# The opening of a macaron block: statistics one tile ahead, the first slot's products by pairs of tiles, lowest parts and router parts ahead of the first multiplication

## The chip, the cores and the metric

One core of one Trainium2 chip. Every time is device time of one launch in microseconds (us), the median of several runs. The kernel before took 1472.89 us (three runs, 1470.03 to 1473.58).

## What is computed

The input `x` is four images of 512 rows by 512 numbers (2048 rows). Two feed-forward blocks stand around an attention block, each behind a layer normalisation and with a residual:

```python
x = x + 0.5 * ffn(layernorm(x), w12, w3, router_w, expert_bias, sw1, sw2, sw3)
x = x + attn(layernorm(x), qkv_w, conv_w0, ..., ln_b)
x = x + 0.5 * ffn(layernorm(x), ...)

def ffn(x, ...):
    shared_out = silu(x @ sw1.T) * (x @ sw2.T) @ sw3.T        # 512 -> 2048 -> 512
    scores = sigmoid(x @ router_w.T)                          # 8 experts
    _, top_idx = top_k(scores + expert_bias, 2)
    # two experts per row, 512 -> 256 -> 512 each, weighted by their scores
    return shared_out + routed_out
```

Here only the start of the first feed-forward block matters: normalising the first four row tiles, splitting the first weights, and the first products of `sw1` and `sw2`.

## The kernel before

**Numbers in two parts.** Products run in bf16, but rows and weights are split into a high and a low bf16 part, and a product takes three passes (high by high, high by low, low by high). For the router a third, lowest part of the rows is made too.

**Slots.** The shared block of one image (512 rows, four tiles of 128) is a unit of 16 slots. A slot does 128 hidden columns: 12 products of 128x128 by 128x512 into `psG` (gate), 12 into `psU` (up), then the 12 products of the slot before with `sw3` into four `psD` banks (`down`). Every engine runs its own program through the slots in the same order and meets the others only at semaphores. Slots below 0 are the preparation; `START` is -7. Slot 0 has no products down.

**One slot, engine by engine.** TensorE (PE): `products` into `psG`, `products` into `psU`, `down` of the slot before; small pieces of the side work (`sides`) stand at six fixed places between them: `pe_third` transposes the third part of a tile, `pe_logits` multiplies by the router. ScalarE (ACT): SiLU of `psG` (L1694), high part of the hidden values (L1704), high parts of rows and weights (`act_split`, L260), copies of side results (L472, L488). VectorE (DVE): the multiplication `sgh = psU * silu` (L1854), statistics, low parts of weights (`vec_split`, L265) and rows. GpSimd (POOL): low part of the hidden values (L1812) and the root of each variance (L520). SP issues nearly all transfers.

**A row tile (class `Prep`)**: `vec_stats` (three VectorE instructions, L508 to L512), `pool_rstd` (L520), `vec_norm` (for tiles 0 to 3 this is `shift`, one small VectorE instruction, L515), `act_norm` (L428), `act_high` (L436), `vec_low` (L440), then SP transposes both parts into `xT` with a DMA (`sp_cross`, L393) and keeps a copy in memory (L399). Later `vec_rest` (L446) and `vec_third` (L455) make the third part, in two VectorE passes. From tile 4 on ScalarE makes the low part (L450) from the rest. `vec_router` splits the router's weights into three parts (L504, L502).

The slots in which a tile goes through its stages stand in the table `TILE`. For tile n below 4: statistics in slot n - 7, shift and high part in n - 6, low part on VectorE in n - 5 (`preps(s - 1, HIGH)`). So VectorE does per slot: shift of one tile, statistics of the next, low part of the one before. Slots -2 and -1 hold the splits of weights 0 (gate, up, down). Then in slot 0, behind the multiplication: statistics of tile 4, router parts, split of weights 1, rest and third parts of tiles 0 and 1; tiles 2 and 3 follow in slot 1.

**TensorE in slot 0** waits for all four transposes (`crossed`) and for the gate's split, does the gate's 12 products on 512 columns each, waits for the up split, and does the other 12. In slot 1, behind the up products, `sides` wants the third part of tile 0 ahead of `down`.

**Transfers.** SP's order after the fourth transpose: weights 1 (two transfers), rows of tiles 4 and 5, the four kept copies, the first expert's weights, the store of the split weights 0, weights 2. In slot 1 it waits for the side piece of tile 0 before it loads the rows of tile 6. Weights 0 are issued by ScalarE's queue at the start.

## Time and profile before

| | |
|---|---|
| median of three runs | 1472.89 us |
| span of the profiled execution | 1469.7 us, the figure of its page |
| lowest run | 1470.03 us |
| TensorE busy | 1419.1 us (97%) |
| VectorE busy | 944.8 us (64%) |
| ScalarE busy | 552.4 us (38%) |
| GpSimd busy | 501.0 us (34%) |
| granted TensorE clock, mean | 0.998 |
| first product | 17.65 us after the start |

The span runs from the first to the last instruction of one execution; what lies around it is not in the trace, and the lowest of the three runs is 0.3 us above it. Busy times of different engines overlap. A time in a timeline counts from the start of the span. In the chain that ended last TensorE holds 63% and VectorE 10%.

### The profile page before, as it was taken

How to read it: one execution, taken by the hardware profiler on the slowest of the kernel's cores; microseconds unless marked ns; L12 is line 12 of the kernel's file. 1: busy time of each engine (PE TensorE's matmuls, PEld its weight loads, DVE VectorE, ACT ScalarE, POOL GpSimd, SP SyncE). 2: the span in 40 equal slices, each digit the busy share in tenths (PEclk: the TensorE clock that was granted, in tenths of full speed). 3: DMA queues.
4: the chain of work that ended last, by engine and by line, in shares of the span. 5: the costliest groups of instructions: out<-in, count | busy, mean ns of one | idle time of the engine just before them, and what ended most of it. 6: DMA issues, size and time to landing. Idle time of an engine off the chain costs nothing.

```text
span 1469.7 us, 22015 instructions
## 1 busy us (share of the span) xinstructions
PE 1419.1 (97%) x7642; PEld 679.7 (46%) x7642; DVE 944.8 (64%) x1295; ACT 552.4 (38%) x1153; POOL 501.0 (34%) x424
## 2 busy tenths in 40 slices
PE   4999999999999999899999999999999999999998
PEld 2444444444444544445454444444444444444443
DVE  5778853333348989898889889979925733333243
ACT  4566323333233433345435454345233213333211
POOL 2321132221244475252625434444322122221353
PEclk9999999999999999999999999999999999999999
DMA  8999659887493467075526552445338168888594
GB/s 305 305 350 320 267 146 209 200 182 192 172 277 125 156 196 220 30 244 135 153 72 186 150 166 73 121 160 140 112 101 257 59 188 213 192 190 185 187 321 165
DMA packets 233724, 272.63 MB, mean 186 GB/s; under 512 B 132242, under 2 KB 156818, under 8 KB 230162
## 3 DMA queue, kind: packets, MB, share of 16 engines
q1 hardware_dynamic: 198594, 166.34, 39.7%
q10 hardware_dynamic: 23664, 67.66, 14.5%
q0 software_dynamic: 11360, 37.23, 9.4%
q8 instruction: 66, 1.08, 0.3%
q14 instruction: 40, 0.33, 0.1%
HBM read 168.39 MB, written 72.88 MB: 164 GB/s over the span
## 4 chain that ended last, share of the span: by engine, by line
PE 63%; DVE 10%; issue 8%; DMA 4%; POOL 2%; ACT 2%; SPq 1%; POOLq 0%; ACTq 0%; DVEq 0%
PE bank L1484 25%; PE bank L1607 13%; PE bank L1498 12%; PE bank L1632 7%; DVE region L1147 3%; DMA rows<-sorted_y,slots 1%; PE side L1120 1%; PE side L1620 1%; DVE region L1153 1%; POOL rows L665 1%; DMA x2d<-rows 1%; DVE sgh L1854 1%; PE side L1253 1%; DMA region<-region 1%; POOL hs L1812 1%
## 5 line engine op out<-in xcount | busy, mean ns | idle before, releaser
L1484 PE MATMUL bank<-xT,wb 128*128 128x512 bf16 x2688 | 615.5, 381 | 22.6 <-DMA xT<-region 17.6
L1484 PEld LDWEIGHTS bank<-xT,wb 128*128 128x128 bf16 x2688 | 257.7, 98 | 323.9 <-issue 29.2
L1812 POOL TENSOR_TENSOR hs<-sgh,hs 128x512 bf16<-128x512 f32 x126 | 161.9, 1285 | 629.1 <-ACT hs L1704 628.2
L1498 PE MATMUL bank<-wb,hs 128*128 128x512 bf16 x1536 | 358.0, 380 | 0.2 <-POOL hs L1812 0.2
L1498 PEld LDWEIGHTS bank<-wb,hs 128*128 128x128 bf16 x1536 | 147.8, 98 | 173.9 <-issue 2.9
L1607 PE MATMUL bank<-wr,region 128*128 x912 | 221.7, 379 | 0.0
L1704 ACT ACTIVATE hs<-sgh 128x512 bf16<-128x512 f32 x128 | 81.3, 635 | 340.2 <-DVE sgh L1854 337.4
L1854 DVE TENSOR_TENSOR sgh<-bank,sgh 128x512 f32<-128x512 f32 x128 | 87.9, 687 | 155.8 <-PE bank L1484 154.6
L1147 DVE TENSOR_TENSOR region<-region 128x1024 f32<-128x1024 f32 x128 | 183.0, 1454 | 0.9
L1801 POOL DMA_INDIRECT region<-xnd,idxs x78 | 74.6, 957 | 221.8 <-DMA region<-region 213.5
L1153 DVE TENSOR_REDUCE region<-region 128x256 f32<-128x2048 f32 x64 | 146.3, 2286 | 2.2
L1694 ACT ACTIVATE sgh<-bank 128x512 f32<-128x512 f32 x128 | 76.4, 597 | 183.3 <-PE bank L1484 164.3
L1607 PEld LDWEIGHTS bank<-wr,region 128*128 128x128 bf16 x912 | 86.0, 98 | 89.8 <-issue 0.7
L1632 PE MATMUL bank<-wr,region 128*128 x468 | 113.7, 379 | 0.0
L1951 DVE TENSOR_TENSOR region<-bank,region 128x256 f32<-128x256 f32 x76 | 32.3, 425 | 97.8 <-ACT region L1742 88.7
L665 POOL DMA_INDIRECT rows<-sorted_y,slots x64 | 67.9, 1062 | 78.5 <-issue 73.4
L1742 ACT ACTIVATE region<-bank 128x256 f32<-128x256 f32 x76 | 29.2, 384 | 172.2 <-PE bank L1607 167.8
L1484 PE MATMUL bank<-region,wb 128*128 128x512 bf16 x384 | 85.9, 379 | 1.9 <-DVE sgh L1854 1.9
L1961 DVE COPY region<-side 128x512 bf16<-128x512 bf16 x78 | 33.1, 425 | 83.5 <-PE side L1620 83.5
L1632 PEld LDWEIGHTS bank<-wr,region 128*128 128x128 bf16 x468 | 45.8, 98 | 55.2
L686 DVE SCALAR_TENSOR_TENSOR rows<-rows,coef 128x512 f32<-128x512 f32 x32 | 26.2, 820 | 68.7 <-DMA rows<-sorted_y,slots 28.3
L1484 PEld LDWEIGHTS bank<-region,wb 128*128 128x128 bf16 x384 | 37.4, 98 | 47.3 <-DVE sgh L1854 2.4
(182 smaller groups left out, 1351.6 us busy)
## 6 DMA issues: line engine op xcount, KB each, us to landing
wb<-wsplit ACTq DMA_DIRECT2D x42, 1024.0 KB
wb<-wsplit ACTq DMA_DIRECT2D x42, 512.0 KB, 4.4
sorted_y<-region SPq DMA_DIRECT2D x78, 256.0 KB
wsplit<-wb SPq DMA_DIRECT2D x8, 1536.0 KB, 7.4
wr<-wall SPq DMA_DIRECT2D x6, 1536.0 KB, 9.7
rows<-x SPq DMA_DIRECT2D x32, 256.0 KB, 4.9
region<-xln SPq DMA_DIRECT2D x128, 64.0 KB, 3.7
xnd<-rows SPq DMA_DIRECT2D x30, 256.0 KB, 4.0
```

The lines of the kernel that those rows point to most:

```text
L665: e.indirect_dma_start(out=dst, out_offset=None, in_=sorted_y, in_offset=bass.IndirectOffsetOnAxis(ap=slots[:, self.f, k, self.t:self.t + ...
L1147: o.do(e.tensor_tensor(t, few.to_broadcast(full), many.to_broadcast(full), ALU.mult))
L1153: o.do(e.tensor_reduce(dst[:, (k - 1) * P:(k + 1) * P], self.tmp.rearrange("p (n c) -> p n c", c=H), AX.X, ALU.add))
L1484: m = e.matmul(ps[:], wb[:, w % 2, wp, at:at + P], xt[:, xp, c, :], start=(i == 0), stop=(i == 3 * NDC - 1))
L1498: m = e.matmul(psD[tt][:], hs[:, s % 2, hp, tt * P:(tt + 1) * P], wb[:, w % 2, wp, at:at + D], start=(first and i == 0), stop=(last and i ...
L1607: m = e.matmul(psH_of(k)[:], xsT[k % RX][:, xp * D + c * P:xp * D + (c + 1) * P], words_of(k, wp, c * D), start=(n == 0), stop=(n == 3 * N ...
L1632: m = e.matmul(psY[k % 2][:], hT[k % 2][:, hp, kt, :], words_of(k, wp, at), start=(n == 0), stop=(n == 3 * KT - 1))
L1694: e.activation(sgh[:, s % 2, :], psG[:], ACT.Silu).then_inc(S("h_silu").sem, 1)
L1704: e.activation(hs[:, s % 2, 0, :], sgh[:, s % 2, :], ACT.Copy).then_inc(S("h_hi").sem, 1)
L1801: e.indirect_dma_start(out=xs[k % RX], out_offset=None, in_=xnd, in_offset=bass.IndirectOffsetOnAxis(ap=idxs[:, k:k + 1], axis=0)).then_in ...
L1812: e.tensor_tensor(hs[:, s % 2, 1, :], sgh[:, s % 2, :], hs[:, s % 2, 0, :], ALU.subtract).then_inc(S("h_lo").sem, 1)
L1854: e.tensor_tensor(sgh[:, s % 2, :], psU[:], sgh[:, s % 2, :], ALU.mult).then_inc(S("h_mul").sem, 1)
```

## The change

It touches TensorE's and VectorE's programs only. TensorE gets `opening()` in the place of slot 0: for gate and up, the products of tiles 0 and 1 (256 columns), then those of tiles 2 and 3, each pair with its own wait for the transposes (once, with the gate) and 12 matmuls; the waits for the splits stay. That makes 48 matmuls of 256 columns out of 24 of 512. VectorE gets `opening()` in the place of the slots below 0: the statistics of tile n + 1 stand ahead of the shift of tile n (tile 3's behind the shift of tile 2), and the rest and third parts of tiles 0 and 1 and the router parts stand behind the splits of weights 0, ahead of slot 0's multiplication, no longer in slot 0. The slots of ScalarE, GpSimd and SP are unchanged.

```diff
--- before.py
+++ after.py
@@ -1486,6 +1486,24 @@
                             i += 1
                     m.then_inc(S(name).sem, 1)
 
+                def opening():
+
+                    for gu, ps, name in ((0, psG, "h_g"), (1, psU, "h_u")):
+                        e.wait_ge(S("w_low").sem, split_done("gu"[gu], 0))
+                        for pair in range(2):
+                            two = slice(2 * pair * P, 2 * (pair + 1) * P)
+                            if gu == 0:
+                                for n in (2 * pair, 2 * pair + 1):
+                                    crossed(e, n)
+                            i = 0
+                            for c in range(NDC):
+                                for wp, xp in PASSES:
+                                    at = gu * NDC * HC + c * HC
+                                    m = e.matmul(ps[:, two], wb[:, 0, wp, at:at + P], xT[0][:, xp, c, two],
+                                                 start=(i == 0), stop=(i == 3 * NDC - 1), skip_group_check=True)
+                                    i += 1
+                        m.then_inc(S(name).sem, 1)
+
                 def down(s, tt):
                     w, k = chunk(s), s % 2
                     first, last = s == 0 or s in EV_AT, s + 1 in EV_AT
@@ -1542,6 +1560,9 @@
                         for pos in range(6):
                             sides(s, pos)
                         return
+                    if s == 0:
+                        opening()
+                        return
                     if s % UNIT == 0:
                         for n in range(4 * u, 4 * u + 4):
                             crossed(e, n)
@@ -1549,25 +1570,22 @@
                             e.wait_ge(S("x_moved").sem, 16 * (u - 1))
                     if s % 2 == 0:
                         if s < UNIT:
-                            e.wait_ge(S("w_low").sem, split_done("gu" if s else "g", chunk(s)))
+                            e.wait_ge(S("w_low").sem, split_done("gu", chunk(s)))
                         elif s % UNIT >= 2 * KT:
                             q, v = chunk_loaded(u, s % UNIT // KT)
                             e.wait_ge(S(f"gu_loaded{q}").sem, v)
                     if s in ROUTED_AT:
                         e.wait_ge(S("r_mul").sem, NB * (ROUTED_AT.index(s) + 1) - 1)
-                    elif s:
+                    else:
                         e.wait_ge(S("h_silu").sem, s)
                     products(psG, s, 0, "h_g", 0)
                     if s in ROUTED_AT:
                         block[ROUTED_AT.index(s)][0](NB - 1)
                     sides(s, 1)
-                    if s == 0:
-                        e.wait_ge(S("w_low").sem, split_done("u", 0))
-                    else:
-                        e.wait_ge(S("h_mul").sem, s)
+                    e.wait_ge(S("h_mul").sem, s)
                     products(psU, s, 1, "h_u", 2)
                     sides(s, 3)
-                    behind = s > 0 and s not in ROUTED_AT
+                    behind = s not in ROUTED_AT
                     if behind:
                         down_ready(s - 1)
                         down(s - 1, 0)
@@ -1847,11 +1865,32 @@
                 e.wait_ge(S("ident_ready").sem, 1)
                 routing = [None, None]
 
+                def opening():
+
+                    tiles = [Prep(n) for n in range(4)]
+                    tiles[0].vec_stats(e, o)
+                    tiles[1].vec_stats(e, o)
+                    tiles[0].vec_norm(e)
+                    tiles[2].vec_stats(e, o)
+                    tiles[1].vec_norm(e)
+                    tiles[0].vec_low(e)
+                    tiles[2].vec_norm(e)
+                    tiles[3].vec_stats(e, o)
+                    tiles[1].vec_low(e)
+                    tiles[3].vec_norm(e)
+                    tiles[2].vec_low(e)
+                    tiles[3].vec_low(e)
+                    for kind in ("g", "u", "down"):
+                        vec_split(e, kind, 0)
+                    for n in range(2):
+                        tiles[n].vec_rest(e)
+                        tiles[n].vec_third(e)
+                    vec_router(e)
+
                 def slot(s):
-                    if s >= 0:
-                        e.wait_ge(S("h_silu").sem, s + 1)
-                        e.wait_ge(S("h_u").sem, s + 1)
-                        e.tensor_tensor(sgh[:, s % 2, :], psU[:], sgh[:, s % 2, :], ALU.mult).then_inc(S("h_mul").sem, 1)
+                    e.wait_ge(S("h_silu").sem, s + 1)
+                    e.wait_ge(S("h_u").sem, s + 1)
+                    e.tensor_tensor(sgh[:, s % 2, :], psU[:], sgh[:, s % 2, :], ALU.mult).then_inc(S("h_mul").sem, 1)
                     if s in ROUTED_AT:
                         e.wait_ge(S("h_hi").sem, s + 1)
                         e.tensor_tensor(hs[:, s % 2, 1, :], sgh[:, s % 2, :], hs[:, s % 2, 0, :],
@@ -1885,24 +1924,17 @@
                     for c in combines(s):
                         if c.ln:
                             c.vec_norm(e)
-                    for p in preps(s - 1, HIGH):
-                        if p.n < 4:
-                            p.vec_low(e)
-                    if s == 0:
-                        vec_router(e)
-                    if s >= 0:
-                        for p in preps(s, LOW):
-                            if p.early:
-                                p.vec_rest(e)
+                    for p in preps(s, LOW):
+                        if p.early:
+                            p.vec_rest(e)
                     for kind, n in splits_at(s)[:1]:
                         vec_split(e, kind, n)
-                    if s >= 0:
-                        for p in preps(s, LOW):
-                            if p.early:
-                                p.vec_third(e)
+                    for p in preps(s, LOW):
+                        if p.early:
+                            p.vec_third(e)
                     for kind, n in splits_at(s)[1:]:
                         vec_split(e, kind, n)
-                    for n in (0, 1) if s == 0 else (2, 3) if s == 1 else ():
+                    for n in (2, 3) if s == 1 else ():
                         Prep(n).vec_rest(e)
                         Prep(n).vec_third(e)
                     for f in range(2):
@@ -1967,7 +1999,8 @@
                         hidden(k)
                     hidden_T(NB - 1)
 
-                for s in range(START, SLOTS_ALL):
+                opening()
+                for s in range(SLOTS_ALL):
                     if s in ROUTED_AT:
                         routed(ROUTED_AT.index(s))
                     slot(s)
```

## Rows read from the trace of the kernel before

**Rows 1.** The page: busy time of TensorE, and its costliest group of weight loads

```profile
...
PE 1419.1 (97%) x7642; PEld 679.7 (46%) x7642; DVE 944.8 (64%) x1295; ACT 552.4 (38%) x1153; POOL 501.0 (34%) x424
...
L1484 PEld LDWEIGHTS bank<-xT,wb 128*128 128x128 bf16 x2688 | 257.7, 98 | 323.9 <-issue 29.2
...
```

**Rows 2.** Waits of TensorE, 0 to 47 us: total, times, longest

```profile
...
PE side L481 <- ACT rows L472: 2.1, 1, 2.1
PE side L463 <- DVE rows L455: 2.1, 1, 2.1
```

**Rows 3.** Timeline of all engines: start, duration, instruction [idle before, releaser]

```profile
...
3.79 0.69 DVE L508 BATCH_NORM_STATS2 stats<-rows 128x6 f32<-128x512 f32 x1 [3.79 <-DMA rows<-x]
...
4.74 0.15 DVE L512 TENSOR_SCALAR mv<-mv 128x1 f32<-128x1 f32 x1
4.98 0.57 POOL L520 TENSOR_TENSOR rstd<-mv,nhalf 128x1 f32<-128x1 f32 x1 [3.19 <-DVE mv L512]
5.59 0.16 DVE L515 SCALAR_TENSOR_TENSOR mv<-mv,rstd 128x1 f32<-128x1 f32 x1 [0.69 <-POOL rstd L520]
...
8.53 0.68 DVE L440 TENSOR_TENSOR rows<-rows 128x512 bf16<-128x512 f32 x1
8.69 0.93 POOL L520 TENSOR_TENSOR rstd<-mv,nhalf 128x1 f32<-128x1 f32 x1 [1.29 <-DVE mv L512]
...
11.87 0.16 DVE L515 SCALAR_TENSOR_TENSOR mv<-mv,rstd 128x1 f32<-128x1 f32 x1 [0.44 <-POOL rstd L520]
...
12.06 0.81 ACT L428 ACTIVATE rows<-rows,mv,rstd 128x512 f32<-128x512 f32 x1 [0.74 <-DVE mv L515]
12.74 2.78 SPq L393 DMA_TRANSPOSE xT<-region  x2
...
13.45 2.93 ACT L260 ACTIVATE wb<-region 128x1024 bf16<-128x1024 f32 x3
13.57 0.69 DVE L440 TENSOR_TENSOR region<-rows,region 128x512 bf16<-128x512 f32 x1 [0.94 <-ACT region L436]
14.52 3.50 DVE L265 TENSOR_TENSOR wb<-region,wb 128x1024 bf16<-128x1024 f32 x3 [0.25 <-ACT wb L260]
...
17.65 12.64 PE L1484 MATMUL bank<-xT,wb 128*128 128x512 bf16 x48 [17.65 <-DMA xT<-region]
...
```

**Rows 4.** The same timeline: weight loads of the first products

```profile
...
18.03 0.15 PEld L1484 LDWEIGHTS bank<-xT,wb 128*128 128x128 bf16 x1 [0.27 <-issue]
...
21.87 7.92 PEld L1484 LDWEIGHTS bank<-xT,wb 128*128 128x128 bf16 x37 [0.28 <-issue]
...
```

**Rows 5.** The same timeline: slots 0 to 2

```profile
...
25.21 0.69 DVE L1854 TENSOR_TENSOR sgh<-bank,sgh 128x512 f32<-128x512 f32 x1 [7.20 <-PE bank L1484]
...
28.64 2.28 DVE L265 TENSOR_TENSOR wb<-region,wb 128x2048 bf16<-128x2048 f32 x1
...
33.50 0.68 DVE L1854 TENSOR_TENSOR sgh<-bank,sgh 128x512 f32<-128x512 f32 x1
...
35.51 1.45 PE L1484 MATMUL bank<-xT,wb 128*128 128x512 bf16 x6
...
41.48 0.69 DVE L1854 TENSOR_TENSOR sgh<-bank,sgh 128x512 f32<-128x512 f32 x1 [1.67 <-PE bank L1484]
...
43.26 1.89 ACT L260 ACTIVATE wb<-region 128x2048 bf16<-128x2048 f32 x1
...
43.55 1.07 DVE L446 TENSOR_TENSOR rows<-rows 128x512 f32<-128x512 f32 x1
...
45.06 0.61 ACT L450 ACTIVATE rows<-rows 128x512 bf16<-128x512 f32 x1
...
```

**Rows 6.** Transfers issued from 22.7 to 23.4 us: size, us to landing

```profile
...
region<-wall SPq DMA_DIRECT2D x1, 512.0 KB, 16.4
```

**Rows 7.** Transfers issued from 32.7 to 33.1 us (tile 6)

```profile
...
rows<-x SPq DMA_DIRECT2D x1, 256.0 KB, 7.0
```

**Rows 8.** Timeline of VectorE, from 75 us: statistics of tile 10

```profile
...
81.18 0.69 DVE L508 BATCH_NORM_STATS2 stats<-rows 128x6 f32<-128x512 f32 x1 [2.11 <-issue]
...
```

## The prediction

> **What bounds the kernel now.** I read the page first: TensorE is busy for 1419.1 of 1469.7 us [rows 1], so the time is its idle time plus its work, and only what moves TensorE counts. The waits of TensorE in the first 47 us came second: 2.1 us for the third part of a row tile (L463) and 2.1 us for ScalarE's copy of one (L472) [rows 2], beside the 17.65 us until the first product, whose row shows it waiting for a transpose [rows 3]. That is 21.9 of some 50 us of idle time, and the change touches all three. Then I read the timeline of that stretch on each engine [rows 3, 5], the weight loads of the first products, for the clock [rows 4], and the landing of the transfers that could come late next [rows 6 to 8].
>
> **The opening up to the first product.** Each of the four tiles goes VectorE statistics, GpSimd root, VectorE shift, ScalarE normalise and high part, VectorE low part, transpose by SP. The statistics take 1.03 us (3.79 to 4.74, and 0.08 until the next can start); the root then holds VectorE up for 0.69 us [rows 3]. Now the next tile's statistics fill that wait. Followed with these rows:
> - Statistics 0 from 3.79, 1 from 4.82, shift 0 at 5.84 instead of 5.59: the first tile is 0.25 us later, ScalarE starts at about 6.03 (0.19 after a shift, as 11.87 to 12.06). GpSimd, ScalarE and SP keep the order of their own work; each only meets its waits earlier.
> - Normalise and high part hold ScalarE for 1.39 us (12.06 to 13.45). Shifts 1 and 2 fall at 6.94 and 8.15, so ScalarE runs 6.03, 7.42, 8.81 with no gap.
> - VectorE: low part 0 at 7.54 (1.51 after its normalise, as 12.06 to 13.57), statistics 3 from 8.23, low part 1 at 9.25. Root 3 starts beside low part 1 and takes 0.93 instead of 0.57 us, as the one at 8.69 did beside the low part at 8.53; shift 3 falls at 10.38, normalise 3 at 10.58 instead of 12.06.
>
> So the last low part and the three weight splits come 1.48 us earlier: 12.09 and, on VectorE, 13.04 instead of 13.57 and 14.52. If root 2, which starts 0.45 us ahead of low part 0, is held up by it too, this shrinks to 1.0 us; above 1.5 us nothing is left, since ScalarE has no gap. I take 1.48: root 2 has most of its 0.57 us behind it by then.
>
> Products by pairs. Now TensorE waits for all four transposes: the last issue is at 14.29 (12.74 + 2.78 - 1.23) and the first product at 17.65, 3.36 later [rows 3]. With pairs it needs tiles 0 and 1 (low part 1 done at 9.94, issued 9.97, landed about 13.3) and the first split (13.04 + 3.50/3 = 14.2). Start: 14.27. The second pair is needed 12 half products later, 16.8; tile 3 is issued at 12.8 and lands at 16.1. Gain at the start: 1.48 + 1.90 = 3.38 us.
>
> Cost of halving: 24 products of 512 columns become 48 of 256. The slot's 24 products took 4.22 + 14 x 0.216 = 7.25 us, 7.29 with the change of clock, and still do if the clock rises 4.2 us after the start again. The first slot ends at 21.6 instead of 24.9.
>
> **What moves ahead of the first multiplication on VectorE.** Rest and third parts of tiles 0 and 1 took 2.6 us (from the split's end, 30.92, to the next multiplication, 33.50), the router parts up to 1.8 us (28.64 - 25.21 less the multiplication and one set of statistics) [rows 5]. They now follow the splits, 16.55 to about 20.9, with VectorE idle there before, and end 0.9 us ahead of the multiplication at 21.8, which waits for TensorE. If the cover goes, the multiplication is late one for one, but the second slot's first half (2.6 us) stands between it and TensorE. Behind it: statistics of tile 4, whose rows had landed by 25.8 and now 1.5 earlier, then the split of the second weights, 3.43 us after the multiplication as before, 25.2 to 27.5. Second multiplication at 27.5. TensorE: slot 1's 24 products take 5.2 us and end at 26.74. Before, they ended at 30.1 and slot 2 began at 35.51; of these 5.4 us 2.3 are the wait for the third part with its restart, 3.1 are work (transposes, products down, logits). The third part is ready from 18 on, so slot 2 starts at 29.85. **Difference 5.66 us** = 3.38 + 2.28 (the wait and its restart). Slot 2 needs the split by then: 2.3 us spare. Its parts 2 and 3 are ready at about 33.7, before TensorE asks.
>
> **Slot 2, where I take some back.** The third wait is a chain behind the multiplication at 41.48: ScalarE high part, weight split (43.26), low part of tile 4 (45.06), copy, TensorE at about 46.3 [rows 2, 5]. It stays, 5.66 earlier, if nothing else is late. VectorE reaches the statistics of tile 6 at 36.9. That tile's load was issued at about 32.8 and landed 7.0 later, 39.8 [rows 7], 0.7 us behind the second part of weights 2 (22.7 + 16.4 = 39.1) [rows 6]. Those weights are issued 1.48 earlier and land at 37.6, early enough for the split at 37.6; the tile's load, though issued at 27.4, stands behind them: 38.3. Statistics end at 39.3, rest part 4 at 40.0 (0.7 like a low part; its 1.07 at 43.55 began beside GpSimd's work, which is over by then), and ScalarE, free at 39.4, starts the low part at 40.0: **0.62 us lost**. If the load took 7.0 us from its issue it would land at 34.4 and nothing would be lost; if it stayed at 39.8, 2.1 us would be.
>
> The Trainium skill, DMA: Bandwidth & Descriptors, section Queues, rings and completion order, says that each engine takes one queue's descriptors in ring order: by that the sum loses the 0.62 us, without it nothing. The 0.7 us between the two landings is what speaks here for order.
>
> **Sum.** 3.38 + 2.28 - 0.62 = 5.04 us earlier at slot 3. From there TensorE is nearly without idle time, and what follows hangs on the slots. The new waits are those of the pairs; behind them on TensorE stand only the same products. Against the profiled execution: span 1469.7 - 5.0 = 1464.7. The three runs have the median 1472.9, 3.2 above that span; I subtract from the median: 1467.9.
>
> **Rivals.**
> 1. *A later clock.* The price is half of each further us at 1.2 GHz; if all 28 remaining half products run low, 28 x 0.107 = 3.0 us, gain 2.0, 1470.9. For it: an earlier start with shorter products. Against: 4.2 us of dense work was enough in [rows 4] and is there again. Chance 0.11. The Trainium skill, TensorE: Matmul & The Clock Gate, Part 1, says that the number of products at half rate differs from run to run of one kernel, which is this rival; one trace cannot test it.
> 2. *The transfers set the pace.* Loads come 1.48 us earlier, work 5.0: up to 3.5 us of queue can stand ahead of slot 3. Tile 10's rows already held VectorE for 2.1 us [rows 8], so what is left of it then goes one for one; together with tile 6 at 39.8 the gain is 1.5 to 3.5, 1469.4 to 1471.4. Against: 6 slots in between. Chance 0.14.
> 3. *The pairs do nothing*, since transposes 0 and 1 slow down beside the first weight load and land with the others: 1.90 lost, gain 3.1, 1469.8. Chance 0.07.
> 4. *Slower.* A gap between the pairs (transpose 3 after 16.8) keeps the clock low. The half-rate stretch costs half its length, so from 10.1 us more of it, a rise after 28.6, the gain is gone; if it stays low to the end of slot 2 the loss is 3.0 + 24 x 0.214 + 36 x 0.214 = 15.8, less 5.0: 1483.7. Against: transpose 3 has 0.7 us spare. Chance 0.05.
> 5. *More*: later waits shrink too, or no loss in slot 2, 1465 to 1467.2. Chance 0.06.
>
> **Numbers.** My forecast has 0.57 and by itself 1466.4 to 1469.4. About 0.3% (4.4 us, 1468.5) is what a measurement of this kernel can tell from no change. Of the forecast's 0.57, 0.44 lies beyond that and 0.13 within; with rival 5 faster is 0.50. Rivals 1 to 3 (0.32) and a hundredth of 4 lie within: 0.46. Slower: 0.04. The range leaves out most of 4 and the ends of 1, 2 and 5, and allows for the 3.5 us by which the three runs differ: 1464.5 to 1472.
>
> **What would show it.** First product at 14.3 with starts 0.21 us apart, the first multiplication at 21.8, the last low part at 12.1. TensorE's wait for L455 gone, that for L472 at 2.7 instead of 2.1 us, and VectorE waiting about 1.4 us for tile 6's rows. Tile 10's wait still about 2.1. The prediction is wrong if the first product starts after 15.5, if the half-rate stretch exceeds 5 us, or if a later wait of TensorE grows by over 1 us.

## The result, and the profile after

The kernel after took 1470.78 us (median of 20 runs, 1465.47 to 1473.95) where the kernel before, on the same chips, took 1474.5 us (20 runs, 1469.81 to 1479.72): a ratio of 0.9975, 95% interval [0.9967, 0.9983], 3.7 us or 0.25%. That is beyond chance, but under the 0.3% named ahead. 5.0 us were predicted.

The page of after and its row of cores (TensorE's granted clock averaged over the span), beside [rows 1]:

```profile
span 1470.5 us, 22063 instructions
...
PE 1422.8 (97%) x7666; PEld 683.9 (47%) x7666; DVE 942.7 (64%) x1295; ACT 552.2 (38%) x1153; POOL 497.4 (34%) x424
...
core 0: 1470.5 us, clock 0.995
```

The profiled execution of after is 0.8 us *longer* than that of before (1469.7 us, clock 0.998). Two single executions can't be set against each other at their ends; they can be at the opening, where the change lies. Waits of TensorE in the first 47 us (total, times, longest), beside [rows 2]:

```profile
PE bank L1502 <- DVE wb L265: 14.3, 1, 14.3
PE side L481 <- ACT rows L472: 3.2, 1, 3.2
```

The wait for the third part (L455) is gone, the start comes 3.35 us earlier, and the last wait has grown by 1.1 us. The timeline of the opening, beside [rows 3]:

```profile
4.81 0.69 DVE L508 BATCH_NORM_STATS2 stats<-rows 128x6 f32<-128x512 f32 x1
...
5.82 0.15 DVE L515 SCALAR_TENSOR_TENSOR mv<-mv,rstd 128x1 f32<-128x1 f32 x1
...
7.06 0.55 POOL L520 TENSOR_TENSOR rstd<-mv,nhalf 128x1 f32<-128x1 f32 x1 [0.52 <-DVE mv L512]
...
8.23 3.86 SPq L393 DMA_TRANSPOSE xT<-rows  x2
...
9.36 0.93 POOL L520 TENSOR_TENSOR rstd<-mv,nhalf 128x1 f32<-128x1 f32 x1 [1.76 <-DVE mv L512]
...
10.33 0.16 DVE L515 SCALAR_TENSOR_TENSOR mv<-mv,rstd 128x1 f32<-128x1 f32 x1 [0.44 <-POOL rstd L520]
...
12.03 0.69 DVE L440 TENSOR_TENSOR region<-rows,region 128x512 bf16<-128x512 f32 x1 [0.94 <-ACT region L436]
12.14 2.69 SPq L393 DMA_TRANSPOSE xT<-region  x2
12.98 3.50 DVE L265 TENSOR_TENSOR wb<-region,wb 128x1024 bf16<-128x1024 f32 x3 [0.26 <-ACT wb L260]
...
14.30 5.07 PE L1502 MATMUL bank<-xT,wb 128*128 128x256 bf16 x23 [14.30 <-DVE wb L265]
...
14.87 0.58 SPq L278 DMA_DIRECT2D region<-wall  x1
```

Every VectorE step stands within 0.1 us of the hand-worked schedule (5.84, 10.38, 12.09, 13.04), and so does the first product (14.27): root 3 took its 0.93 us beside a low part, root 2 escaped with 0.55. SP does not follow: two transposes occupied it from 8.23 to 12.09, in before from 9.24 to 12.70, so the first load behind the transposes went out at 14.87, only 0.70 us earlier (15.57 before) instead of 1.48. By the second part of weights 2 SP has made that up (21.21 against 22.72). The first two transposes landed 5.0 and 4.2 us after their issue (3.1 and 3.2 in before), the second at about 14.1, just ahead of the first product.

One thing on the clock. The granted clock reads 1.00 all through this opening, in before too, so its level there is read from the distance of the starts alone. Slots 0 to 3, beside [rows 5]:

```profile
18.43 0.69 DVE L455 TENSOR_TENSOR rows<-rows 128x512 bf16<-128x512 f32 x1
...
22.46 0.69 DVE L1893 TENSOR_TENSOR sgh<-bank,sgh 128x512 f32<-128x512 f32 x1 [2.35 <-PE bank L1502]
...
30.48 1.45 PE L1484 MATMUL bank<-xT,wb 128*128 128x512 bf16 x6
...
36.45 0.69 DVE L1893 TENSOR_TENSOR sgh<-bank,sgh 128x512 f32<-128x512 f32 x1 [2.29 <-PE bank L1484]
...
39.41 0.69 DVE L508 BATCH_NORM_STATS2 stats<-rows 128x6 f32<-128x512 f32 x1 [1.81 <-issue]
...
41.14 0.63 ACT L450 ACTIVATE rows<-rows 128x512 bf16<-128x512 f32 x1 [1.01 <-DVE rows L446]
...
42.40 0.20 PE L481 MATMUL side<-rw,xT 128*128 128x24 bf16 x2 [3.24 <-ACT rows L472]
...
43.90 0.15 PEld L1484 LDWEIGHTS bank<-xT,wb 128*128 128x128 bf16 x1 [0.23 <-issue]
...
44.32 0.15 PEld L1484 LDWEIGHTS bank<-xT,wb 128*128 128x128 bf16 x1 [0.28 <-issue]
...
50.36 0.69 DVE L1893 TENSOR_TENSOR sgh<-bank,sgh 128x512 f32<-128x512 f32 x1 [6.45 <-PE bank L1484]
```

VectorE waits 1.81 us for the rows of tile 6 (39.41), and TensorE 3.24 us for what hangs on them. It goes on at 42.40, 3.9 us ahead of before. Then something unforeseen: from 43.90 its weight loads start 0.42 us apart, the 1.2 GHz level, until 46.88, so the multiplication of slot 3 comes only 2.2 us earlier (50.36 against 52.58). Two transfers, beside [rows 6, 7] (size, us from issue to landing; the weights were issued at 21.21, the rows at 27.78):

```profile
region<-wall SPq DMA_DIRECT2D x1, 512.0 KB, 17.5
...
rows<-x SPq DMA_DIRECT2D x1, 256.0 KB, 11.5
```

They land at 38.7 and 39.3 us, 0.6 us apart (0.7 in before) and only 0.4 and 0.5 us earlier than there. Three later waits:

```profile
79.36 0.20 PE L481 MATMUL side<-rw,xT 128*128 128x24 bf16 x2 [1.17 <-issue]
...
96.57 0.69 DVE L508 BATCH_NORM_STATS2 stats<-rows 128x6 f32<-128x512 f32 x1 [1.80 <-issue]
...
97.48 0.20 PE L481 MATMUL side<-rw,region 128*128 128x24 bf16 x2 [1.38 <-issue]
```

The first is TensorE in slot 6, waiting for the transpose of tile 7, issued at 72.48 and landed 6.8 us later; before has it too (1.34 us). The second is VectorE, waiting 1.80 us for the rows of tile 12 (0.32 in before, though they come 0.9 us earlier now: the work asks 2.4 us earlier). The third is new: TensorE in slot 8, waiting for the transpose of tile 9, issued at 89.15 and landed 8.2 us later (6.8 in before, without a wait). All the way, from the start times of the multiplications in both timelines:

```
multiplication at (before)   25.2   33.5   41.5   52.6   96.0   112.8   182.6
earlier in after by           2.75   5.65   5.0    2.2    2.4     1.1     1.1
```

### The profile page after: what moved, and what is told of

Its sections match the earlier page's. It is cut to its first block, busy times and chain, and to the rows that moved or that the text cites. A ratio compares the mean times of both kernels' runs of the same rounds, so it can differ in the third digit from the quotient of the medians.

```text
span 1470.5 us, 22063 instructions
## 1 busy us (share of the span) xinstructions
PE 1422.8 (97%) x7666; PEld 683.9 (47%) x7666; DVE 942.7 (64%) x1295; ACT 552.2 (38%) x1153; POOL 497.4 (34%) x424
## 4 chain that ended last, share of the span: by engine, by line
PE 64%; DVE 10%; issue 8%; DMA 4%; POOL 2%; ACT 2%; SPq 1%; POOLq 0%; ACTq 0%; DVEq 0%
PE bank L1484 25%; PE bank L1625 13%; PE bank L1516 13%; PE bank L1650 7%; DVE region L1147 3%; DMA rows<-sorted_y,slots 2%; PE side L1120 1%; PE side L1638 1%; DVE region L1153 1%; POOL rows L665 1%; DVE sgh L1893 1%; PE side L1253 1%; DMA region<-region 1%; PE side L1236 1%; DVE rows L578 0%
## 5 line engine op out<-in xcount | busy, mean ns | idle before, releaser
L1484 PE MATMUL bank<-xT,wb 128*128 128x512 bf16 x2664 | 609.4, 380 | 5.2 <-ACT sgh L1712 3.7
L1993 DVE COPY region<-side 128x512 bf16<-128x512 bf16 x78 | 33.1, 425 | 83.7 <-PE side L1638 83.7
```

The costliest lines, as they stand in the source:

```text
L1484: m = e.matmul(ps[:], wb[:, w % 2, wp, at:at + P], xt[:, xp, c, :], start=(i == 0), stop=(i == 3 * NDC - 1))
```

## Experiments

A1 to A4 ask what closes in at the end of slot 2, B1 to B3 undo one part of the change each, C to E follow up what these left open. All were timed against before on the same chip. Ratios are of medians, with their 95% intervals.

**A1. TensorE kept at work.** After, plus twelve products that nobody reads, in the gate's bank, just ahead of the side work it waits with. Nothing is left out.

```diff
                         down(s - 1, 3)
+                    if s == 2:
+                        e.wait_ge(S("h_silu").sem, 3)
+                        for i in range(12):
+                            e.matmul(psG[:], xT[0][:, 0, 0, 0:P], xT[0][:, 0, 0, :], start=(i == 0), stop=(i == 11))
                     sides(s, 5)
```

> The changed kernel with 12 products more that nobody reads, into the gate's bank at the end of slot 2, where TensorE waits 3.2 us for ScalarE's copy of tile 2's third part (12 x 0.216 = 2.6 us, so they end before the wait does). Clock theory (that wait lets TensorE's clock fall for 3.4 us, 1.7 us lost): no stretch at 0.50 near 44 us, the copy still ends the wait near 42.4, slot 3's multiplication on VectorE at 48.7 instead of 50.4, median 1.7 us below the changed kernel, some 0.9963 of the kernel before. Rival (the clock there costs nothing, since slot 3 is held by loads): slot 3's multiplication stays at 50.4, ratio 0.9975.

1469.67 us (12 runs), ratio 0.9969 [0.9958, 0.998]. Stretches of after (us, busy time and instructions of PE, PEld, VectorE, ScalarE, GpSimd; then the granted clock, the DMA's share and GB/s):

```profile
43.90:44.90 1.00, 1.00 (x4) 0.45 (x3) 0.01 (x1) 0.00 (x0) 0.00 (x0) 0.50 0.77 164
44.90:45.90 1.00, 1.00 (x4) 0.30 (x3) 0.00 (x0) 0.00 (x0) 0.00 (x0) 0.50 1.07 263
```

The same of A1, and its TensorE row behind the products:

```profile
43.90:44.90 1.00, 1.00 (x6) 0.49 (x5) 0.13 (x1) 0.00 (x0) 0.00 (x0) 1.00 0.77 161
44.90:45.90 1.00, 1.00 (x10) 0.57 (x8) 0.00 (x0) 0.23 (x1) 0.00 (x0) 1.00 1.12 302
```

```profile
42.52 0.20 PE L481 MATMUL side<-rw,xT 128*128 128x24 bf16 x2 [1.88 <-ACT rows L472]
```

TensorE goes on at the same moment (42.52 against 42.40) but at the full clock, and the multiplication of slot 3 comes at 48.80 instead of 50.36, 6.28 us behind that moment instead of 7.96: the half-rate stretch costs 1.7 us, and no more. That the products kept the clock up isn't shown by one profile; behind B1's wait of 3.13 us, without such products, it stayed up as well. The median lies 1.1 us below after's, within the two intervals.

**A2. Tile 6's rows ahead of weights that aren't needed yet.** SP loads the first expert's weights (1.5 MB) behind those rows; weights 2 stay ahead of them.

```diff
                             Prep(n).sp_keep(e)
-                        load_raw(e, NU)
...
+                    if s == 1:
+                        load_raw(e, NU)
                     for n in raws_at(s):
```

> The changed kernel with the first expert's weights (1.5 MB) issued in slot 1 behind tile 6's rows, instead of ahead of the store of split weights 0. Queue theory (tile 6's rows land late because they stand behind what was issued before): 1.5 MB less ahead of them at 0.4 MB per us, so they land near 35.7 instead of 39.3, before VectorE asks at 37.5; its wait of 1.8 us goes, TensorE's wait at the end of slot 2 falls from 3.2 to 2.1 us, and the fall of the clock with it where the shorter wait is not seen by the clock: 1.1 us, or 2.8 us with the clock, ratio 0.9956 to 0.9967. Rival (the load's own latency under load is what counts): it lands 11 us after its issue as before, nothing moves, 0.9975. Tiles 7 and 10 must not come later than before (VectorE's wait in slot 6 stays 1.9 us).

1468.45 us (6 runs), 0.9954 [0.9939, 0.9969]. Its timeline:

```profile
37.22 0.68 DVE L508 BATCH_NORM_STATS2 stats<-rows 128x6 f32<-128x512 f32 x1
...
40.98 0.20 PE L481 MATMUL side<-rw,xT 128*128 128x24 bf16 x2 [2.11 <-ACT rows L472]
...
47.25 0.69 DVE L1894 TENSOR_TENSOR sgh<-bank,sgh 128x512 f32<-128x512 f32 x1 [4.49 <-PE bank L1485]
```

VectorE no longer waits, TensorE's wait is 2.11 us again, the clock holds. Weights 2 land at 34.7 us (issued at 20.00, 14.7 us) and the rows at 35.3 (27.49, 7.8 us), still 0.6 us behind them. With 1.5 MB less ahead of the rows the late opening of slot 3 goes: what stood ahead of them in the queue was the cap.

**A3. The router products of tile 2 out of TensorE's way**, from slot 2 into slot 3.

```diff
-                logits_at = ((1, 5), (2, 2), (2, 5), (3, 2))[n]
+                logits_at = ((1, 5), (2, 2), (3, 1), (3, 2))[n]
```

> The changed kernel with tile 2's router products moved from the end of slot 2 to behind the gate products of slot 3. If the copy on ScalarE is all that TensorE waits for there, the wait of 3.2 us goes and the clock stays high: slot 3's multiplication comes 3.2 + 1.7 = 4.9 us earlier, at 45.5 instead of 50.4. Transfer theory (the loads then become the bound): part of it comes back as waits of VectorE for the rows of tiles 7, 8 and 10, up to what TensorE has gained, and the median falls by less than 3 us; without it by 4 to 5 us (0.9942 to 0.9948 of the kernel before).

1468.03 us (6 runs), 0.9951 [0.9935, 0.9968]. Its timeline:

```profile
45.48 0.69 DVE L1893 TENSOR_TENSOR sgh<-bank,sgh 128x512 f32<-128x512 f32 x1 [1.95 <-PE bank L1484]
...
57.78 0.69 DVE L508 BATCH_NORM_STATS2 stats<-rows 128x6 f32<-128x512 f32 x1 [2.46 <-issue]
...
58.33 0.20 PE L481 MATMUL side<-rw,xT 128*128 128x24 bf16 x2 [1.85 <-issue]
...
60.04 0.15 PEld L1484 LDWEIGHTS bank<-xT,wb 128*128 128x128 bf16 x1 [0.24 <-issue]
60.47 0.15 PEld L1484 LDWEIGHTS bank<-xT,wb 128*128 128x128 bf16 x1 [0.28 <-issue]
```

The slot-3 multiplication comes 4.9 us ahead of after, as expected (45.5), and two slots on most of it is gone: TensorE waits 1.85 us, and its clock drops behind that (starts 0.43 us apart). In slot 5 the lead over after is 1.4 us. What ends the wait at 58.33 is the transpose of tile 5, issued at 50.40, which lands at 58.2:

```profile
xT<-rows SPq DMA_TRANSPOSE x1, 7.8
```

Tile 8's rows hold VectorE for 2.46 us, but not TensorE: it goes on 0.55 us behind the start of their statistics, where after needed 3.0 us from such a start to what is made from it (39.41 to 42.40).

**A4. Both, A2 and A3.**

> Both moves, of the first expert's load and of tile 2's router products, in the changed kernel. Clock and queue theory together: as with the router products moved alone, and VectorE does not wait for tile 6 in slot 2 either; since TensorE no longer hangs on it there, this adds little over the other (0 to 1 us): 0.994 to 0.995 of the kernel before. If the transfers are the bound from slot 3 on, the gain of both is no more than that of either alone.

1468.9 us (6 runs), 0.9955 [0.9939, 0.9971]. The slot-3 multiplication stands at 44.55. In slot 4 TensorE waits 2.45 us for the transpose of tile 5 (issued at 48.38, landed 9.5 us later), and the clock falls again: no better than either alone. Tile 8's rows, 3.06 us late, hold only VectorE. Under the first cap lies a second, and it is a transpose.

**B1. The statistics back behind the shift** (the rest of the change kept).

```diff
                     tiles[0].vec_stats(e, o)
-                    tiles[1].vec_stats(e, o)
                     tiles[0].vec_norm(e)
-                    tiles[2].vec_stats(e, o)
+                    tiles[1].vec_stats(e, o)
                     tiles[1].vec_norm(e)
+                    tiles[2].vec_stats(e, o)
                     tiles[0].vec_low(e)
```

> The changed kernel with VectorE's statistics back behind the shift of the tile before. Step theory: the last low part and the splits come 1.48 us later again, first product at 15.8 instead of 14.3 us; the loads that SP issues behind the fourth transpose come later too. Clock theory adds that the stretch at half rate behind it differs by run. Slot 3's resume 1.5 us later, unless the wait for tile 6's rows hides it (then less, since those rows move only with SP's loads); median 0 to 1.5 us above the changed kernel, ratio 0.9975 to 0.9985 of the kernel before.

1472.16 us (12 runs), 0.9983 [0.9969, 0.9996]. The first product moves from 14.30 to 15.80, which is the 1.5 us worked out for this part. The end of slot 2 moves from 42.40 to 44.01, since here the loads behind the transposes are later too (the first at 15.53 instead of 14.87).

**B2. No pairs**: all four transposes first, then products of 512 columns.

```diff
-                        for pair in range(2):
-                            two = slice(2 * pair * P, 2 * (pair + 1) * P)
-                            if gu == 0:
-                                for n in (2 * pair, 2 * pair + 1):
-                                    crossed(e, n)
+                        if gu == 0:
+                            for n in range(4):
+                                crossed(e, n)
+                        for pair in range(1):
+                            two = slice(0, 4 * P)
```

> The changed kernel with slot 0's products on 512 columns behind all four transposes. Step theory: first product 3.2 to 3.4 us behind the fourth transpose's issue (13.5 us), near 16.8; slot 2's multiplication 2.5 us later, near 39. Tile 6's rows land at 39.3 either way and are asked for at 40 then, so VectorE's wait of 1.8 us goes, TensorE waits 2.1 instead of 3.2 us at the end of slot 2 and resumes near 43.7, 1.3 us after the changed kernel, not 2.5. If the shorter wait also keeps the clock up, the pairs bring nothing at all: slot 3's multiplication at 50.0 against 50.4, ratio 0.997 to 0.998.

1470.62 us (12 runs), 0.9965 [0.9952, 0.9978]. Its timeline:

```profile
16.62 0.59 PE L1502 MATMUL bank<-xT,wb 128*128 128x512 bf16 x1 [16.62 <-DMA xT<-region]
...
42.95 0.20 PE L481 MATMUL side<-rw,xT 128*128 128x24 bf16 x2 [2.12 <-ACT rows L472]
```

The pairs are worth 2.3 us at the first product and 0.55 at the end of slot 2. The wait there is 2.12 us, the clock doesn't fall, and slot 3's multiplication (49.22) is even ahead of after's. Nothing of the pairs can be seen in the time.

**B3. Rest, third and router parts back in slot 0.**

```diff
                         vec_split(e, kind, 0)
-                    for n in range(2):
-                        tiles[n].vec_rest(e)
-                        tiles[n].vec_third(e)
-                    vec_router(e)
...
+                    if s == 0:
+                        vec_router(e)
...
-                    for n in (2, 3) if s == 1 else ():
+                    for n in (0, 1) if s == 0 else (2, 3) if s == 1 else ():
```

> The changed kernel with the rest and third parts of tiles 0 and 1 and the router parts back in slot 0, behind its multiplication. Step theory: TensorE's wait of 2.1 us for the third part (L455) comes back in slot 1, slot 2 starts 2.3 us later (32.8 instead of 30.5), and slot 2's multiplication comes at 38.7. As with the pairs, the wait for tile 6 then shrinks, so of the 2.3 us some 1.1 us or less are left at the end of slot 2, and with the clock up nothing. Ratio 0.997 to 0.9985; the rival, that every microsecond of slot 2 counts in full, gives 2.3 us above the changed kernel, 0.999.

1471.49 us (12 runs), 0.9977 [0.9963, 0.9991]. Its timeline:

```profile
28.70 0.38 PE L463 MATMUL side<-identb,rows 128*128 128x128 bf16 x4 [2.10 <-DVE rows L455]
...
42.60 0.20 PE L481 MATMUL side<-rw,xT 128*128 128x24 bf16 x2 [2.12 <-ACT rows L472]
```

The 2.1 us wait is back, and yet the end of slot 2 moves by 0.2 us alone: what is won ahead of tile 6's rows is waited away at them. Part of the 0.2 is luck, since the clock rose at 17.7 here and at 20.0 in after; against D3 (18.1, the end at 42.30) it is 0.3.

**C. Tiles 10 to 15 loaded one slot earlier**, on top of A2.

```diff
-            TILE.append((n - 5 if n >= 6 else None, at, ...
+            TILE.append((n - 6 if n >= 10 else n - 5 if n >= 6 else None, at, ...
```

> The changed kernel with the first expert's load behind tile 6's rows, and the rows of tiles 10 to 15 loaded one slot earlier. Queue theory: VectorE's waits for tile 10 (1.9 to 2.1 us) and tile 12 (1.3 to 1.8 us) go, and TensorE's two waits behind them (1.3 and 1.1 us): 2.4 us below the version with the first expert's load alone moved, 0.9935 to 0.9945 of the kernel before. Rival: the queue is full there, so the rows come at the expense of the weights, VectorE or ScalarE waits for those instead, and the ratio stays 0.9954.

1469.42 us (12 runs), 0.9959 [0.9945, 0.9973]. VectorE's waits for tiles 10 and 12 are gone, TensorE's small waits in slots 6 and 8 are not (2.8 us together), and nothing is won over A2. They end when a transpose lands, 7.0, 6.7 and 8.6 us after its issue. So the rows of tile 10 [rows 8] are not what holds TensorE.

**D1. Stores of the split weights on ScalarE's queue**, on top of A2: do the transposes get free of them?

```diff
-                    if 0 <= s < UNIT and s % 2 == 0:
-                        store_split(e, s // 2)
...
                         act_split(e, kind, n)
+                    if 0 <= s < UNIT and s % 2 == 0:
+                        store_split(e, s // 2)
```

> The changed kernel with the first expert's load behind tile 6's rows, and the stores of the split weights issued on ScalarE's queue instead of SP's. TensorE's waits of 1.2 to 1.4 us in slots 6 and 8 end where the DMA transposes of tiles 7 and 9 land, 6.8 and 8.2 us after their issue. Queue theory (a transpose waits for what stands ahead of it on SP's queue): 1.5 MB less ahead, they land in 3 to 5 us, both waits go, 2.4 us below the version with the first expert's load alone moved: 0.9935 to 0.9945 of the kernel before. Rival (all queues share the same 16 engines, so the transposes land no sooner): the waits stay, 0.9954.

1470.75 us (12 runs), 0.9975 [0.9964, 0.9987]: no gain; tile 7's transpose still takes 6.3 us, those of tiles 8 to 10 take 7.5 to 8.0. Its end of slot 2, and a stretch behind it (columns as above):

```profile
40.60 0.20 PE L481 MATMUL side<-rw,xT 128*128 128x24 bf16 x2 [2.12 <-ACT rows L472]
```

```profile
42.00:43.00 1.00, 1.00 (x4) 0.42 (x3) 0.38 (x1) 0.00 (x0) 0.00 (x0) 0.50 0.49 182
```

Here the clock fell behind a wait of only 2.12 us.

**D2. The statistics alone** (B2 and B3 together): are the two parts each other's spare?

> The changed kernel with both the pairs and the early rest, third and router parts undone; only the statistics ahead are left. If tile 6's rows (landed at 39.3) cap slot 2, each of the two parts alone brings TensorE nearly as far as both: it resumed at 42.4 with both, at 42.6 without the early parts, at 42.95 without the pairs. Without both nothing is capped: 1.0 to 1.5 us before the kernel before, at 44.8 to 45.3, slot 3's multiplication at 51.1 to 51.6. Sum theory (parts add): 42.4 + 0.2 + 0.55 = 43.2. Median 1 to 1.5 us below the kernel before, ratio 0.999 to 0.9993.

1472.13 us (12 runs), 0.9982 [0.9971, 0.9994]. Its timeline:

```profile
30.69 0.38 PE L463 MATMUL side<-identb,rows 128*128 128x128 bf16 x4 [2.11 <-DVE rows L455]
...
44.59 0.20 PE L481 MATMUL side<-rw,xT 128*128 128x24 bf16 x2 [2.11 <-ACT rows L472]
```

The end of slot 2 stands at 42.40 with both parts, 42.95 and 42.60 without one, 44.59 without either. Each alone is worth 1.6 to 2.0 us there, both together 2.2: they add almost nothing to each other, because the cap lies at 42.4. The median is 2.6 us below before's, where 1 to 1.5 were expected.

**D3. The kernel after again**, for how much one profile tells.

> The changed kernel once more, on the chip of the others, for a second trace: statistics of tile 6 again held to 39.0 to 39.6 us, TensorE resumes at 42.2 to 42.6. By the clock theory the stretch at half rate behind that wait of 3.2 us comes again (near 44); if it was chance it is not there and slot 3's multiplication comes at 48.7. Tile 12's rows late by over 1 us again, and TensorE's waits at the landing of the transposes of tiles 7 and 9. Ratio 0.9975 within 0.0012.

1470.74 us (12 runs), 0.9975 [0.9963, 0.9987], the first result again. Its timeline:

```profile
42.30 0.20 PE L481 MATMUL side<-rw,xT 128*128 128x24 bf16 x2 [3.89 <-ACT rows L472]
...
43.01 0.15 PEld L1484 LDWEIGHTS bank<-xT,wb 128*128 128x128 bf16 x1 [0.28 <-issue]
43.43 0.15 PEld L1484 LDWEIGHTS bank<-xT,wb 128*128 128x128 bf16 x1 [0.28 <-issue]
```

In the opening the clock rose 1.9 us earlier than in the first profile (18.1 against 20.0), and slot 2's multiplication stood at 35.70 instead of 36.45. But the end of slot 2 is the same (42.30 against 42.40), the wait only longer, and the fall of the clock is there again.

**E. A2 and eight unread products** behind slot 2, nothing left out: does the pair beat both?

> The changed kernel with the first expert's load behind tile 6's rows, and 8 products that nobody reads (1.7 us) in the 2.1 us in which TensorE then waits at the end of slot 2. With both the late rows and the fall of the clock gone: rows of tile 6 never waited for, TensorE resumes 0.6 us behind the last filler where it resumed without them (40.6 to 41.5), no stretch at 0.50 near 42 us, slot 3's multiplication 6.3 us after the resume (46.9 to 47.8), ratio 0.995 (0.9938 to 0.9962), 3 to 4 us below the changed kernel. If the clock falls behind such a wait only now and then (one look in six so far), the fillers add 0.3 us at most over the move alone, 0.9954.

1469.53 us (12 runs), 0.9968 [0.9956, 0.9979], not the 0.995 hoped for. Its opening:

```profile
15.01 8.04 PE L1503 MATMUL bank<-xT,wb 128*128 128x256 bf16 x48 [15.01 <-DMA xT<-rows]
```

The first product waited for a transpose until 15.01, 0.8 us later than A2's (14.25), and the clock rose late (20.6). TensorE went on at 41.98, and slot 3's multiplication came at 48.25, a microsecond behind A2's; the whole microsecond is there at the first multiplication already (23.16 against 22.16). The products fill the wait of 2.1 us down to 0.39; that is worth something only where the clock would have fallen, and in A2 it hadn't. Whether A2's load order is worth anything over after isn't settled either: E contains it and lies 1.3 us below after, C 1.4, D1 nothing, all within each other's intervals.

**The profiles together.** The lead over the profile of before at the multiplication that stands at 182.6 us there (worked out from the start times), the lead of the medians, what the span of each profile adds to its lead behind 182.6 us, and how many half-rate stretches the granted clock shows from 183 us to the last microseconds (before: 2; one of B2's is twice as long and counts as two):

```
                     D2   after  B1   D1   D3   B2   A1   B3   E    C    A3   A4   A2
lead at 182.6 us     0.8  1.1    1.6  1.7  2.0  2.5  3.0  3.1  3.4  3.5  3.9  4.2  4.4
lead of the medians  2.6  3.7    3.2  3.9  4.0  4.8  5.2  3.9  4.8  6.0  6.8  5.9  6.4
behind 182.6 us     -4.3 -1.9   -0.5 -3.1  1.8 -2.1 -2.5 -3.1 -0.8 -0.5 -3.0 -2.7 -1.8
half-rate stretches  3    3      2    3    1    3    3    4    2    2    3    3    2
```

The first two go together (correlation 0.90, slope 0.99, 2.0 us between them). So do the last two (correlation -0.86, 1.8 us for each stretch, beside the 1.7 that A1 gives for one): what moved the single profiles behind 183 us, in code that the change doesn't touch, is mostly how often the clock fell there.

## Why the prediction was right, and where it wasn't

1. **The opening, 3.38 us: right.** First product at 14.30 (14.27 forecast), each VectorE step within 0.1 us. B1 puts 1.5 us on the statistics. B2 gives the pairs 2.3 us of the first product, where 1.9 stood. It was close: the second transpose landed at 14.1, not at 13.3, and in D1 and E TensorE waited for it until 15.0, which is rival 3 in part.
2. **Halving at no cost, clock after 4.2 us: the first held, the second didn't.** The half products start 0.21 us apart at 1.2 GHz. B2, with whole products, needs 7.5 us from the first product to the first multiplication, 4.2 of them at the low clock, and after 8.2, of them 5.7: the 0.7 between them is half of the longer stretch, and nothing is left for the halving. But in the first profile the clock rose 5.7 us after the start instead of 4.2, slot 0 took 8.05 us instead of 7.29, and the first multiplication came at 22.46, not 21.8. That is rival 1, by 0.75 us. It costs nothing in the end: D3, 0.75 us ahead in slot 2, ends it at the same time.
3. **The wait for the third part: right.** It is gone, the moved VectorE work is done at 20.1 us, ahead of the multiplication, and B3 and D2 bring the wait back at 2.1 us.
4. **Tile 6's rows, 0.62 us: right in kind, too small.** They land behind the weights, at 39.3. The term is mis-sized in "those weights are issued 1.48 earlier and land at 37.6". Their second part was issued 1.51 earlier (21.21 against 22.72), but took 17.5 us instead of 16.4 and landed at 38.7, 0.4 earlier. Two transfers ahead of it kept their lead: the first expert's weights landed 1.7 us earlier (19.45 + 10.6 against 20.76 + 11.0), the store of weights 0 1.6. What made weights 2 slower isn't shown. TensorE loses 1.1 us more. That the rows land behind what stands ahead of them in the queue is shown: 0.7 us behind weights 2 in before and 0.6 in after, D3 and A2, from 7.0 to 12.2 us after their own issue. The Trainium skill, DMA: Bandwidth & Descriptors, section Queues, rings and completion order, has an engine consume descriptors in ring order. The trace agrees with that.
5. **"What follows hangs on the slots": wrong.** The longer wait at the end of slot 2 is followed by a half-rate stretch in both profiles of after (1.7 us by A1). I had put the risk of the clock into the opening, not behind the wait that the change itself makes longer. It isn't certain: the clock fell behind 3.24 and 3.89 us, not behind B1's 3.13; behind waits of about 2.1 us at that place it fell in one of seven profiles (D1), and stayed up in before, A2, B2, B3, C and D2. Two slots on it fell behind 1.85 us (A3) and 2.45 us (A4).
6. **Rival 2, later loads: it happened, in part.** Slots 8 to 10 give 1.3 us back, nearly all of it in the new wait of 1.38 us at 97.48. My reading of [rows 8] was wrong: it is a wait of VectorE that TensorE doesn't feel (C). TensorE's own waits there, and in slot 4 of A3 and A4, end where a transpose lands; the prediction has no transpose behind the opening.
7. **The sum.** 5.04 less 1.1 (tile 6), 1.7 (clock) and 1.1 (net, behind slot 3) is 1.1, the lead in the first profile at 182.6 us. The medians lie 3.7 apart. The profile of before is a quick one: its span of 1469.7 us stands for a launch of about 1471.4 (in every timed run the launch time is 1.7 to 1.8 us above the span), 3.1 below the median of 1474.5. Whether the 2.0 us between the two kinds of lead are luck that it already had at 182.6 us, or whether the other kernels win them behind that, one profile of before can't show. So 1470.78 falls inside the range of 1464.5 to 1472.0, but outside the likeliest case's own (1466.4 to 1469.4), near what rivals 1 and 2 gave. Of the 2.9 us above the forecast of 1467.9, 1.6 come from its base, since the median of three runs (1472.89) was 1474.5 in twenty, and 1.3 from the gain. The gain was forecast beyond 0.3% with chance 0.50 and within it with 0.46; it lies within.
8. **Its own signs of being wrong.** Of the three that it names, the first didn't come (the first product started at 14.3). The other two did: the half-rate stretch was 5.7 us in the first profile (3.7 in D3), over the 5 named, and the wait for L472 grew by 1.1 us, over the 1 named, beside the new wait of 1.38. The total held better than the account of what follows slot 2, and that part of it is luck.

That slot 3 comes only 2.2 us earlier is therefore mostly a cap: the pairs and the early third parts win 1.6 to 2.0 us each alone, and 2.2 together. The rest of what they win is waited away at tile 6's rows, and behind that wait the clock fell in both profiles of after.

**Open**: why weights 2 took 1.1 us longer to land; why tile 12's rows gained only 0.9 us; what decides whether the clock falls behind a wait; whether A2 or A3 beats after by more than chance (six runs each; their intervals overlap after's). The cap behind A4, the landing of a transpose, was not taken away.

## What to carry to other kernels

Work out an early gain up to the next load that is late, by its place in the queue, and stop adding there: two edits that both end under the same cap are worth one. A wait that grows on TensorE costs its length and sometimes a half-rate stretch behind it as well, so look for the clock in the slot after the wait and not only at the start. When two engines wait at about the same time, ask what ended each wait: a late load on VectorE and a late transpose on TensorE looked like one cause in A3, and weren't. And a single profile may be some microseconds from its median: compare early landmarks in several profiles, count the half-rate stretches behind them, and compare the ends over many runs.

## What the runs showed of the hardware

- A DMA transpose, landed 3.1 to 3.4 us after its issue in before's opening, took 5.0 and 4.2 us when issued a microsecond or more earlier, beside the weight loads. Beside loads and stores it took 7.8 us (A3, issued at 50.40), 9.5 us (A4, issued at 48.38), and 4.3 to 8.2 us between 72 and 100 us in after. SP itself was held in issuing the second for 2.18 us instead of 1.24. Moving the stores to another issuing engine didn't help (D1: 6.3 to 8.0 us). The Trainium skill, DMA: Bandwidth & Descriptors, section Issuing engines are not separate DMA queues, says that whichever engine starts them, transfers run on the same 16 DMA engines and interleave; D1 agrees, as far as one run can.
- The clock rose at 17.5 to 21.7 us in the profiles of the changed kernels, whose first product starts at 14.2 to 16.6 us. The Trainium skill, TensorE: Matmul & The Clock Gate, Part 1, calls the number of half-rate products variable from run to run; the first profile of after and D3, one kernel, agree (20.0 and 18.1).
- One wait of TensorE near 1060 us (L1236) lasts 2.26 or 2.27 us in all fourteen profiles. The clock fell behind it in eleven, and not in before, B2 and D3. Stretches of 1062 to 1070 us, before and then after (the granted clock is the third number from the end):

```profile
1062.00:1070.00 8.00, 5.74 (x36) 3.08 (x36) 3.02 (x5) 2.03 (x4) 1.16 (x1) 1.00 0.12 49
```

```profile
1062.00:1070.00 8.00, 5.82 (x24) 3.15 (x25) 2.56 (x4) 1.79 (x3) 1.15 (x1) 0.79 0.06 23
```

- Over the runs the mean granted clock and the time go together: correlation -0.87 over the 98 runs of before that were timed beside the experiments and -0.81 over 20 of after, about 1.6 us for each 0.001. So most of the spread of 8 to 10 us goes with the clock.
